# Units of a scan run by halves of the channels, with one PSUM bank for the state sum and two for B

## The chip, the core and the metric

The kernel is one program on one core of a Trainium2 chip. The core has five instruction streams that run side by side and wait for each other through semaphores: TensorE (PE, matrix products into PSUM), VectorE (DVE), ScalarE (ACT), GpSimd (POOL) and SyncE (SP, which here only starts transfers). PSUM has eight banks of 128 partitions x 512 f32. The metric is the device time of one execution in microseconds (us), less is better.

## The reference

Input x is 8 sequences of 256 tokens with 128 features. After a layer norm two branches run on it, and the output is x + s * g.

```python
x = L0_attn_x
xn = _layernorm(x, axis=-1)
s = _L0_attn_ref(xn, ...)            # the selective scan
g = _silu(_L0_ffn_ref(xn, ...))      # mixture of 8 experts, the best 2 of each token
x = x + s * g
...
# inside _L0_attn_ref: DIN = 256 channels, S = 16 states, R = 64
xz = xn @ W_in
xi, z = jnp.split(xz, 2, axis=-1)
...                                   # causal convolution of 4 taps, then silu, gives xc
dt, Bm, Cm = jnp.split(xc @ W_x, [R, R + S], axis=-1)
dt = jax.nn.softplus(dt @ W_dt + b_dt)
dA = jnp.exp(dt[..., None] * A)
dBu = (dt * xc)[..., None] * Bm[:, :, None, :]
...                                   # h = dA * h + dBu along the tokens
y = jnp.einsum('blds,bls->bld', h, Cm) + D_skip * xc
y = y * jax.nn.silu(z)
return x + y @ W_out
```

## The kernel before

**Tiling.** The 2048 tokens are cut into 4 chunks of 512 tokens (two sequences). Within a chunk the scan works on tiles of 128 partitions that hold 4 states of 32 channels. There are 8 blocks of 32 channels and 4 quads of states, so 32 such tiles in a chunk. Two neighbouring blocks make a pair, and one quad of one pair is a *unit*: 16 units in a chunk, 64 in all. Unit n belongs to chunk n // 16; `place(n)` (L101) gives its quad and its pair. Before, the pair runs fastest: the four pairs of quad 0, then the four pairs of quad 1, and so on.

**What a unit is.** ACT makes the decay `dec` = exp(dt * A) (L448, two instructions). DVE multiplies `rep` (dt * u of these channels, repeated over the four states) with B of this quad, which lies in a PSUM bank `pB` (L726, `times_B`), and runs the scan (L735) into `hs`. POOL multiplies with C (L358, two instructions) into `hc`; PE adds the four states up into the bank of the channels, `py` (L837, `reduce`, for two units at a time), after a product of xc with D_skip has opened the sum (L826, `skip_xc`). When all units of a chunk are added, DVE multiplies `py` with silu(z) (L744, `gate_y`), and PE multiplies with W_out (L920, job "o").

**Around it** lie the jobs of the next chunk's front (transpose "tr", convolution "xc0", "xc1", gate input "z0", "z1", the product "dt", then "v0", "v1" for dt, the softplus on ACT, DVE and POOL, and the normalised input "tn"), and the eight experts of the mixture: "m" jobs (L908), "y" jobs (L914), emptied by ACT (L531) and added by POOL (L411), a few of them by DVE (L761: expert 4 of chunk 2 and experts 6 and 7 of chunk 3). The router of the mixture is a chain of small DVE instructions (L668 to L696) that ends in `score`; job "gs" on PE (L896) waits for it, and job "gb" and the expert outputs stand behind it.

**The order is written out by hand.** Every engine runs through the same numbered slots: slot 2n is `times_B` of unit n on DVE and slot 2n+1 its scan; a chunk is 32 slots. The tables FIRST, MIDDLE, LAST and STEPS say in which slot of a chunk which job or DVE step is issued; "slot 16 of chunk 1" below means 16 slots after the chunk's first. Each engine is strictly in order, so what waits holds up all that stands behind it. PE runs `reduce` six slots after the units that it adds (LAG).

**Banks.** `pB` has one bank, `pdbu` (the output of `times_B`) two, `py` two (one for each half of the channels), the jobs three. B of a quad is spread by one PE product (L816, `spread_B`), which must wait until DVE has made the last `times_B` of the quad before, and the next `times_B` waits for it.

**The repeated rows.** `rep` has one buffer. SP writes it by 32 transfers a chunk (L336), eight for each pair, as soon as the last quad of the old chunk has read that pair, and only once dt * u of all 256 channels is there (`far_done`, released by the memset at L716). Ahead of them SP writes the C rows out and reads them back in (L318, L323). ACT and DVE wait for a pair's transfers at its first quad.

**The end.** After the last scan DVE adds the two last experts' outputs, with `gate_y` of chunk 3 between them; then come "o" on PE and three DVE instructions (L754, L797, L799).

## Time and profile before

| | |
|---|---|
| runs (3) | median 395.79 us, 393.49 to 396.25 |
| the profiled execution | 393.58 us |
| its span in the profile | 391.6 us |
| mean granted TensorE clock | 0.873 of full |
| busy | PE 287.7 us, DVE 314.6, ACT 214.2, POOL 228.1 |

The profile follows one execution. Its span runs from the first to the last instruction and is 2.0 us shorter than that execution's own time. Times in rows are microseconds from the start of the span. A share of busy time is a mean over stages with different limits; whether a stage is bound by an engine is read from the waits in it.

### The profile page before, as it was taken

Reading aid. Unit: us, or ns where it says so; the run is one execution under the profiler, and the core shown is the slowest. Engines: PE = TensorE matmul, PEld = TensorE weight load, DVE = VectorE, ACT = ScalarE, POOL = GpSimd, SP = SyncE. Lnnn points to the kernel's source line nnn. Section 1 sums busy time; section 2 is a strip of 40 time slices with the busy share of each in tenths; the row PEclk is TensorE's granted clock in tenths of the full one; section 3 lists DMA queues with packets and bytes.
Section 4 is the critical chain, followed back from the end, with each engine's and each line's share of the span. In section 5 each row is a group of like instructions: output and inputs, shape, how many; then the busy total and the mean of one; then the engine's idle time right before and its main releaser. Section 6 shows DMA issues by size and latency. Waiting matters only on the chain. (4 is left out here: it accounts for less than half of the span.)

```text
span 391.6 us, 4141 instructions
## 1 busy us (share of the span) xinstructions
PE 287.7 (73%) x1191; PEld 147.4 (38%) x1191; DVE 314.6 (80%) x374; ACT 214.2 (55%) x405; POOL 228.1 (58%) x197
## 2 busy tenths in 40 slices
PE   0847077969258878877669969877489869698884
PEld 0313043424224354224426445224236346063453
DVE  3772378693999899997897998997985998999955
ACT  1271264597444744588627664589526563656840
POOL 3050221853953965646757866546946676769880
PEclk9986569978688999988969978989859998879999
DMA  6945940004003870004004950003003980000001
GB/s 179 263 104 122 206 109 2 1 0 110 1 1 74 200 157 2 1 10 100 2 1 102 206 122 1 1 20 92 0 2 79 205 202 0 0 0 2 0 0 55
DMA packets 16755, 26.74 MB, mean 68 GB/s; under 512 B 4263, under 2 KB 9758, under 8 KB 16734
## 3 DMA queue, kind: packets, MB, share of 16 engines
q1 hardware_dynamic: 16438, 25.96, 28.4%
q10 hardware_dynamic: 296, 0.53, 0.4%
q8 instruction: 10, 0.16, 0.2%
q14 instruction: 11, 0.09, 0.1%
HBM read 8.52 MB, written 1.18 MB: 25 GB/s over the span
## 5 line engine op out<-in xcount | busy, mean ns | idle before, releaser
L358 POOL TENSOR_TENSOR hc<-hs,Ct 128x512 f32<-128x512 f32 x126 | 160.2, 1295 | 72.3 <-DVE hs L735 72.3
L735 DVE TENSOR_TENSOR_SCAN hs<-dec,pdbu 128x1024 f32<-128x1024 f32 x64 | 146.2, 2284 | 4.5
L448 ACT ACTIVATE dec<-rep,negA 128x512 f32<-128x512 f32 x128 | 88.6, 722 | 42.3 <-DMA rep<-dt_u 30.6
L726 DVE TENSOR_TENSOR pdbu<-rep,pB 128x1024 f32<-128x1024 f32 x64 | 78.5, 1227 | 32.3 <-PE pB L816 21.1
L908 PE MATMUL px<-xnT,w 128*128 128x512 f32 x128 | 71.8, 668 | 17.2 <-ACT hT L542 13.6
L914 PEld LDWEIGHTS px<-w,hT 128*128 128x128 f32 x512 | 68.3, 212 | 29.0 <-issue 12.3
L914 PE MATMUL px<-w,hT 128*128 128x128 f32 x512 | 70.9, 298 | 9.5 <-DVE glc L669 7.5
L411 POOL TENSOR_TENSOR acc<-acc,ysc 128x512 f32<-128x512 f32 x29 | 37.5, 1292 | 47.7 <-ACT ysc L531 38.8
L542 ACT ACTIVATE hT<-px,cols 128x512 f32<-128x512 f32 x64 | 43.7, 689 | 22.5 <-PE px L908 19.1
L531 ACT ACTIVATE ysc<-px,score 128x128 f32<-128x128 f32 x116 | 33.1, 367 | 39.5 <-PE px L914 36.7
L837 PE MATMUL py<-hc,rsel 128*32 128x512 f32 x256 | 47.5, 668 | 8.2 <-POOL hc L358 8.2
L908 PEld LDWEIGHTS px<-xnT,w 128*128 128x128 f32 x128 | 23.7, 210 | 47.1 <-issue 20.7
L873 PE MATMUL px<-xrT,wtap 128*128 128x512 f32 x56 | 27.1, 614 | 0.0
L816 PE MATMUL pB<-dtp,sel 128*128 128x512 f32 x32 | 19.9, 706 | 6.7 <-DVE pdbu L726 6.7
L880 PE MATMUL px<-xc,wx 128*96 128x512 f32 x16 | 12.1, 900 | 11.4 <-ACT xc L464 11.4
L837 PEld LDWEIGHTS py<-hc,rsel 128*32 128x32 f32 x256 | 6.6, 113 | 36.0 <-POOL hc L358 23.1
L920 PE MATMUL px<-wout,sz 128*128 128x128 f32 x64 | 11.9, 362 | 9.8 <-DVE sz L744 9.8
L873 PEld LDWEIGHTS px<-xrT,wtap 128*128 128x128 f32 x56 | 10.5, 196 | 15.7 <-issue 13.2
L920 PEld LDWEIGHTS px<-wout,sz 128*128 128x128 f32 x64 | 11.0, 267 | 11.7 <-issue 7.3
L365 POOL TENSOR_TENSOR zr<-zr,xv 128x512 f32<-128x512 f32 x6 | 7.8, 1294 | 12.2 <-DVE xv L707 12.2
L816 PEld LDWEIGHTS pB<-dtp,sel 128*128 128x128 f32 x32 | 5.9, 207 | 20.3 <-issue 12.8
L704 DVE TENSOR_SCALAR xv<-ev 128x512 f32<-128x512 f32 x8 | 4.4, 552 | 9.9 <-ACT ev L473 9.8
(103 smaller groups left out, 251.0 us busy)
## 6 DMA issues: line engine op xcount, KB each, us to landing
rep<-dt_u SPq DMA_DIRECT2D x128, 128.0 KB, 2.4
Ct<-c_rows SPq DMA_DIRECT2D x16, 256.0 KB, 4.7
w<-in_L_ffn_W SPq DMA_DIRECT2D x1, 1024.0 KB
out<-xn SPq DMA_DIRECT2D x4, 256.0 KB, 3.2
x_sb<-in_L_attn_x SPq DMA_DIRECT2D x1, 768.0 KB, 5.4
hc<-in_L_attn_conv_w ACTq DMA_DIRECT2D x1, 512.0 KB, 4.3
x_sb<-in_L_attn_x SPq DMA_DIRECT2D x1, 256.0 KB, 5.4
win<-in_L_attn_W_in SPq DMA_DIRECT2D x1, 256.0 KB, 4.7
```

The lines of the kernel that those rows point to most:

```text
L358: eng.tensor_tensor(hc[:, n % HC_RING, i, :], hs[:, n % HS_RING, i, :], Ct[:, k % 2, j, :], ALU.mult).then_inc(hc_last if n == UNITS - 1 e ...
L411: pool.tensor_tensor(acc[:, k % 3, :], acc[:, k % 3, :], ysc[:, :], ALU.add).then_inc(acc_added, 1)
L448: act.activation(dec[:, n % DEC_RING, i, :], rep[:, q, 0, :], ACT.Exp, scale=negA[:, q, j:j + 1])\
L531: ins = act.activation(ysc[:, t], src[:, t], ACT.Copy, scale=score[:, k % 2, i, e:e + 1])
L542: ins = act.activation(hT[:, e % 2, b, :], src[:, :], ACT.Relu, bias=cols[:, V_B1 + HB * e + b:V_B1 + HB * e + b + 1])
L726: dve.tensor_tensor(pdbu[:, :, :], rep[:, 2 * pair:2 * pair + 2, 1, :], pB[:, :, :].to_broadcast([P, 2, CH]), ALU.mult).then_inc(dbu_done, 1)
L735: dve.tensor_tensor_scan(hs[:, n % HS_RING].rearrange("p b t -> p (b t)"), dec[:, n % DEC_RING].rearrange("p b t -> p (b t)"), pdbu[:, :, ...
L816: pe.matmul(pB[:, 0, :], sel[:, j].rearrange("p s d -> p (s d)"), dtp[:, k % 2, :], start=True, stop=True)\
L837: last = pe.matmul(py[r:r + GD, b, :], rsel[:, :], hc[:, n % HC_RING, i, :], start=False, stop=j == QUADS - 1)
L873: last = pe.matmul(dst[:, :], wtap[:, t, b * P:(b + 1) * P], xrT[:, :, t:t + SEQ], start=t == 0, stop=t == TAPS - 1)
L908: last = pe.matmul(dst[:, :], w1[:, e, b * P:(b + 1) * P], xnT[:, k % 2, :], start=True, stop=True)
L914: last = pe.matmul(dst[:, i * D:(i + 1) * D], hT[:, e % 2, b, i * P:(i + 1) * P], w2[:, e, b, :], start=b == 0, stop=b == HB - 1)
```

## The change

The units of a chunk are put in another order: first the four quads of states over pairs 0 and 1 (channels 0 to 127), then the four quads over pairs 2 and 3. With it:

- one `py` bank holds the sum of the half that is being worked on; it is opened by one L826 product for each half and read by one `gate_y` for each half, in slots 20 and 36 instead of one in slot 35. A line that is now issued for the second half waits until `gate_y` of the first half has read the bank;
- the bank that came free goes to `pB`, which has two. B is spread for every two units instead of every four (32 instead of 16 products), and one turn earlier: the product for the units from slot 4i+8 on stands in slot 4i+3;
- the memset that releases `far_done` is made for each half, and SP asks for each pair only for its own half; pairs 0 and 1 are free for the next chunk after the 8th unit, pairs 2 and 3 after the 16th.

The line numbers in rows are those of the kernel before; after the change the same instructions stand at L820 (`spread_B`), L828, L839, L748 (`gate_y`), L719 (memset).

```diff
@@ -29,6 +29,8 @@
 BLOCKS = DIN // GD
 PAIRS = BLOCKS // 2
 PER_CHUNK = QUADS * PAIRS
+PER_HALF = PER_CHUNK // DB
+HALF_PAIRS = PAIRS // DB
 UNITS = CHUNKS * PER_CHUNK
 HALF = 2 * PER_CHUNK
 DEC_RING, HS_RING, HC_RING = 3, 3, 4
@@ -75,14 +77,14 @@
 
 STEPS = [{
     "silu": [13], "log1p": [15, 15], "correct": [16, 16, 16, 16], "sum_dt": [15, 15], "times_dt": [18, 21],
-    "scale_rows": [4], "normalise": [14], "gate": [19, 20, 20, 20, 21, 21], "gate_e": [19], "gate_y": [35],
+    "scale_rows": [4], "normalise": [14], "gate": [19, 20, 20, 20, 21, 21], "gate_e": [19], "gate_y": [20, 36],
 }, {
     "silu": [12], "log1p": [15, 15], "correct": [16, 16, 17, 19], "sum_dt": [16, 20], "times_dt": [18, 21],
     "scale_rows": [4], "normalise": [11], "gate": [19, 20, 20, 20, 20, 20], "gate_e": [20], "finish": [20],
-    "gate_y": [35],
+    "gate_y": [20, 36],
 }]
 START = {"gate": [1, 1, 1, 3, 3, 3], "gate_e": [0]}
-END = {"gate_y": [35]}
+END = {"gate_y": [20, 36]}
 LEAD = 2
 LAG = 6
 
@@ -100,7 +102,8 @@
 
 def place(n):
 
-    return n // PER_CHUNK, n // PAIRS % QUADS, n % PAIRS
+    k, b = n // PER_CHUNK, n // PER_HALF % DB
+    return k, n // HALF_PAIRS % QUADS, HALF_PAIRS * b + n % HALF_PAIRS
 
 
 def by_dve(job, k):
@@ -204,9 +207,9 @@
         def banks(name, n):
             return ctx.enter_context(nc.psum_tensor(name, [P, n, CH], F32))
 
-        pB = banks("pB", 1)
+        pB = banks("pB", 2)
         pdbu = banks("pdbu", 2)
-        py = banks("py", DB)
+        py = banks("py", 1)
         px = [banks(f"px{i}", 1)[:, 0, :] for i in range(AUX)]
 
 
@@ -326,8 +329,10 @@
 
             def repeat_dt_u(k, pair):
 
+                sp.wait_ge(far_done, DB * k + pair // HALF_PAIRS + 1)
                 if k > 0:
-                    free = PER_CHUNK * (k - 1) + PAIRS * (QUADS - 1) + pair + 1
+                    b = pair // HALF_PAIRS
+                    free = PER_CHUNK * (k - 1) + PER_HALF * (b + 1) - HALF_PAIRS + pair % HALF_PAIRS + 1
                     sp.wait_ge(decay_done, 2 * free)
                     sp.wait_ge(dbu_done, free)
                 for q in (2 * pair, 2 * pair + 1):
@@ -337,7 +342,6 @@
 
             for k in range(CHUNKS):
                 repeat_C(k)
-                sp.wait_ge(far_done, k + 1)
                 for pair in range(PAIRS):
                     repeat_dt_u(k, pair)
             for k in range(CHUNKS):
@@ -507,7 +511,7 @@
                 elif job == "dt":
                     if k >= 2:
                         act.wait_ge(c_out, 16 * (k - 1))
-                        act.wait_ge(B_spread, QUADS * (k - 1))
+                        act.wait_ge(B_spread, DB * QUADS * (k - 1))
                     ins = act.activation(dtp[0:RANK + 2 * STATES, k % 2, :], src[0:RANK + 2 * STATES, :], ACT.Copy)
                 elif job in ("v0", "v1"):
                     b = int(job[1])
@@ -711,19 +715,19 @@
                 dve.wait_ge(dt_done, DB * k + b + 1)
                 wait_silu(dve, "xc", k, b)
                 dve.tensor_tensor(dt_u[:, b, 1, :], dt_u[:, b, 0, :], xc[:, k % 2, b], ALU.mult).then_inc(u_done, 1)
-                if b == DB - 1:
-                    dve.wait_ge(u_done, DB * (k + 1))
-                    dve.memset(dt_u[:, :, 0, 0:CH:SEQ], FAR).then_inc(far_done, 1)
+                dve.wait_ge(u_done, DB * k + b + 1)
+                dve.memset(dt_u[:, b, 0, 0:CH:SEQ], FAR).then_inc(far_done, 1)
 
             def times_B(n):
 
                 k, j, pair = place(n)
-                dve.wait_ge(B_spread, n // PAIRS + 1)
+                m = n // HALF_PAIRS
+                dve.wait_ge(B_spread, m + 1)
                 if j == 0:
                     dve.wait_ge(rep_in[pair], N_REP * (k + 1))
                 if n > 0:
                     dve.wait_ge(scan_done, n)
-                dve.tensor_tensor(pdbu[:, :, :], rep[:, 2 * pair:2 * pair + 2, 1, :], pB[:, :, :].to_broadcast([P, 2, CH]),
+                dve.tensor_tensor(pdbu[:, :, :], rep[:, 2 * pair:2 * pair + 2, 1, :], pB[:, m % 2:m % 2 + 1, :].to_broadcast([P, 2, CH]),
                                   ALU.mult).then_inc(dbu_done, 1)
 
             def scan(n):
@@ -737,11 +741,11 @@
                                        pdbu[:, :, :].rearrange("p b t -> p (b t)"), 0.0, ALU.mult, ALU.add)\
                     .then_inc(scan_done, 1)
 
-            def gate_y(k):
-
-                dve.wait_ge(reduced, PER_CHUNK // 2 * (k + 1))
-                wait_silu(dve, "z", k, DB - 1)
-                dve.tensor_tensor(sz[:, k % 2], py[:, :, :], sz[:, k % 2], ALU.mult).then_inc(yg_done, 1)
+            def gate_y(k, b):
+
+                dve.wait_ge(reduced, (PER_CHUNK * k + PER_HALF * (b + 1)) // 2)
+                wait_silu(dve, "z", k, b)
+                dve.tensor_tensor(sz[:, k % 2, b], py[:, 0, :], sz[:, k % 2, b], ALU.mult).then_inc(yg_done, 1)
 
             def empty(job, k):
 
@@ -776,8 +780,8 @@
                     scan(n // 2) if n % 2 else times_B(n // 2)
                 if n == 2 * UNITS - 1:
                     times_C(dve, UNITS - 1)
-                for k, _ in steps_at(n, "gate_y"):
-                    gate_y(k - 1)
+                for k, b in steps_at(n, "gate_y"):
+                    gate_y(k - 1, b)
                 for k, _ in steps_at(n, "scale_rows"):
                     scale_rows(k)
                 for k, _ in steps_at(n, "normalise"):
@@ -808,33 +812,31 @@
 
             def spread_B(m):
 
-                k, j = m // QUADS, m % QUADS
+                k, j = m // (DB * QUADS), m % QUADS
+                if m % (DB * QUADS) == 0:
+                    wait_emptied(pe, "dt", k)
+                if m > 1:
+                    pe.wait_ge(dbu_done, HALF_PAIRS * (m - 1))
+                pe.matmul(pB[:, m % 2, :], sel[:, j].rearrange("p s d -> p (s d)"), dtp[:, k % 2, :], start=True, stop=True)\
+                    .then_inc(B_spread, 1)
+
+            def skip_xc(k, b):
+
+                wait_silu(pe, "xc", k, b)
+                if DB * k + b > 0:
+                    pe.wait_ge(yg_done, DB * k + b)
+                pe.matmul(py[:, 0, :], skip[:, b, :], xc[:, k % 2, b, :], start=True, stop=False)
+
+            def reduce(m):
+
+                k, j, pair = place(2 * m)
                 if j == 0:
-                    wait_emptied(pe, "dt", k)
-                if m > 0:
-                    pe.wait_ge(dbu_done, PAIRS * m)
-                pe.matmul(pB[:, 0, :], sel[:, j].rearrange("p s d -> p (s d)"), dtp[:, k % 2, :], start=True, stop=True)\
-                    .then_inc(B_spread, 1)
-
-            def skip_xc(k):
-
-                for b in range(DB):
-                    wait_silu(pe, "xc", k, b)
-                if k > 0:
-                    pe.wait_ge(yg_done, k)
-                for b in range(DB):
-                    pe.matmul(py[:, b, :], skip[:, b, :], xc[:, k % 2, b, :], start=True, stop=False)
-
-            def reduce(m):
-
-                k, j, pair = place(2 * m)
-                if j == 0 and pair == 0:
-                    skip_xc(k)
+                    skip_xc(k, pair // HALF_PAIRS)
                 for n in (2 * m, 2 * m + 1):
                     pe.wait_ge(hc_last, 2) if n == UNITS - 1 else pe.wait_ge(hc_done, 2 * (n + 1))
                     for i in range(2):
-                        b, r = divmod((2 * (n % PAIRS) + i) * GD, P)
-                        last = pe.matmul(py[r:r + GD, b, :], rsel[:, :], hc[:, n % HC_RING, i, :], start=False,
+                        r = (2 * n + i) * GD % P
+                        last = pe.matmul(py[r:r + GD, 0, :], rsel[:, :], hc[:, n % HC_RING, i, :], start=False,
                                          stop=j == QUADS - 1)
                 last.then_inc(reduced, 1)
 
@@ -914,8 +916,8 @@
                             last = pe.matmul(dst[:, i * D:(i + 1) * D], hT[:, e % 2, b, i * P:(i + 1) * P], w2[:, e, b, :],
                                              start=b == 0, stop=b == HB - 1)
                 else:
-                    pe.wait_ge(yg_done, k + 1)
                     for b in range(DB):
+                        pe.wait_ge(yg_done, DB * k + b + 1)
                         for i in range(TPC):
                             last = pe.matmul(dst[:, i * D:(i + 1) * D], sz[:, k % 2, b, i * P:(i + 1) * P], wout[:, b, :],
                                              start=b + i == 0, stop=(b, i) == (DB - 1, TPC - 1))
@@ -927,9 +929,10 @@
             pe.wait_ge(setup, N_SETUP)
             pe.wait_ge(vec_c, 1)
             spread_B(0)
+            spread_B(1)
             for n in range(END_SLOT + 1):
-                if n % (2 * PAIRS) == 2 * PAIRS - 1 and n // (2 * PAIRS) + 1 < CHUNKS * QUADS:
-                    spread_B(n // (2 * PAIRS) + 1)
+                if n % 4 == 3 and n // 4 + 2 < UNITS // HALF_PAIRS:
+                    spread_B(n // 4 + 2)
                 if n % 4 == 2 and 0 <= (n - LAG) // 4 < UNITS // 2:
                     reduce((n - LAG) // 4)
                 for job, k in SLOTS.get(n, []):
```

Three places of the resulting order. On DVE at the start, before the first unit (dt_u<-dt_u,xc is dt * u of a half), before:

```order
L713 TENSOR_TENSOR dt_u<-dt_u,xc 128x512
L704 TENSOR_SCALAR xv<-ev 128x512
L707 TENSOR_TENSOR xv<-xv,ev 128x512
L365 TENSOR_TENSOR zr<-zr,xv 128x512
L371 TENSOR_TENSOR dt_u<-zr,rl 128x512
L713 TENSOR_TENSOR dt_u<-dt_u,xc 128x512
L716 MEMSET dt_u 128x2x2
```

and after the change:

```order
L717 TENSOR_TENSOR dt_u<-dt_u,xc 128x512
L719 MEMSET dt_u 128x2
L708 TENSOR_SCALAR xv<-ev 128x512
L711 TENSOR_TENSOR xv<-xv,ev 128x512
L369 TENSOR_TENSOR zr<-zr,xv 128x512
L375 TENSOR_TENSOR dt_u<-zr,rl 128x512
L717 TENSOR_TENSOR dt_u<-dt_u,xc 128x512
L719 MEMSET dt_u 128x2
```

The memset of the first half has moved ahead of the five instructions of the second half.

On PE in chunks 1 and 2, from the transpose of `score` (job "gs") to the expert product "y4"; before:

```order
L896 MATMUL px2<-ident,score 32x128
L837 MATMUL py<-hc,rsel 32x512 x4
L908 MATMUL px0<-xnT,w1 128x512
L902 MATMUL px1<-b2d,sT 128x512
L914 MATMUL px2<-w2,hT 128x128 x8
L908 MATMUL px0<-xnT,w1 128x512
L816 MATMUL pB<-dtp,sel 128x512
L914 MATMUL px1<-w2,hT 128x128 x8
```

and after:

```order
L898 MATMUL px2<-ident,score 32x128
L828 MATMUL py<-xc,skip 128x512
L839 MATMUL py<-hc,rsel 32x512 x4
L910 MATMUL px0<-xnT,w1 128x512
L904 MATMUL px1<-b2d,sT 128x512
L916 MATMUL px2<-w2,hT 128x128 x8
L910 MATMUL px0<-xnT,w1 128x512
L820 MATMUL pB<-dtp,sel 128x512
L916 MATMUL px1<-w2,hT 128x128 x8
```

The product with D_skip of the second half stands between `score` and the expert outputs now, and the spread at this place serves units two turns later; another spread (slot 27) stands a little further on, ahead of y4.

On DVE at the very end, before:

```order
L358 TENSOR_TENSOR hc<-hs,Ct 128x512 x2
L761 SCALAR_TENSOR_TENSOR acc<-px,score,acc 128x128 x4
L744 TENSOR_TENSOR sz<-py,sz 128x1024
L761 SCALAR_TENSOR_TENSOR acc<-px,score,acc 128x128 x4
L754 TENSOR_TENSOR xn<-px,xn 128x512
```

and after:

```order
L362 TENSOR_TENSOR hc<-hs,Ct 128x512 x2
L765 SCALAR_TENSOR_TENSOR acc<-px,score,acc 128x128 x8
L748 TENSOR_TENSOR sz<-py,sz 128x512
L758 TENSOR_TENSOR xn<-px,xn 128x512
L801 TENSOR_TENSOR xn<-xn,acc 128x512
```

The last `gate_y` is half as wide and stands behind both expert sums instead of between them.

## Rows read from the trace of the kernel before

**Rows 1.** Page, busy time, share of the span and instructions of each engine
```profile
PE 287.7 (73%) x1191; PEld 147.4 (38%) x1191; DVE 314.6 (80%) x374; ACT 214.2 (55%) x405; POOL 228.1 (58%) x197
```

**Rows 2.** Waits of the run: total us, times, longest us
```profile
ACT dec L448 <- DMA rep<-dt_u: 30.6, 12, 6.9
...
DVE pdbu L726 <- PE pB L816: 21.1, 10, 5.2
```

**Rows 3.** Timeline, DVE, the start: start us, duration us, instruction, [idle before <- releaser]
```profile
28.41 0.69 DVE L713 TENSOR_TENSOR dt_u<-dt_u,xc 128x512 f32<-128x512 f32 x1
...
32.48 0.06 DVE L716 MEMSET dt_u<- 128x4 f32 x1
39.61 1.23 DVE L726 TENSOR_TENSOR pdbu<-rep,pB 128x1024 f32<-128x1024 f32 x1 [7.06 <-DMA rep<-dt_u]
...
50.55 0.19 DVE L673 TENSOR_REDUCE gsm<-gex 128x4 f32<-128x32 f32 x1 [6.99 <-ACT gex L549]
```

**Rows 4.** Timeline, ACT, the start
```profile
44.58 1.33 ACT L448 ACTIVATE dec<-rep,negA 128x512 f32<-128x512 f32 x2 [3.65 <-DMA rep<-dt_u]
...
50.31 0.21 ACT L549 ACTIVATE gex<-glc 128x32 f32<-128x32 f32 x1
```

**Rows 5.** Timeline, DVE, chunk 0 and the first unit of chunk 1
```profile
92.00 1.23 DVE L726 TENSOR_TENSOR pdbu<-rep,pB 128x1024 f32<-128x1024 f32 x1 [3.93 <-PE pB L816]
95.84 0.43 DVE L704 TENSOR_SCALAR xv<-ev 128x512 f32<-128x512 f32 x1 [2.60 <-ACT ev L473]
...
136.29 1.23 DVE L726 TENSOR_TENSOR pdbu<-rep,pB 128x1024 f32<-128x1024 f32 x1 [1.36 <-PE pB L816]
```

**Rows 6.** Timeline, PE, chunk 1: a spread, the reduce of slot 18
```profile
155.82 1.02 PE L816 MATMUL pB<-dtp,sel 128*128 128x512 f32 x2
...
182.11 1.29 PE L837 MATMUL py<-hc,rsel 128*32 128x512 f32 x8
```

**Rows 7.** Timeline, DVE, chunk 1
```profile
178.47 0.43 DVE L704 TENSOR_SCALAR xv<-ev 128x512 f32<-128x512 f32 x1 [2.60 <-ACT ev L473]
...
188.52 1.22 DVE L726 TENSOR_TENSOR pdbu<-rep,pB 128x1024 f32<-128x1024 f32 x1
...
208.05 1.23 DVE L726 TENSOR_TENSOR pdbu<-rep,pB 128x1024 f32<-128x1024 f32 x1 [2.62 <-PE pB L816]
...
230.19 1.20 DVE L744 TENSOR_TENSOR sz<-py,sz 128x1024 f32<-128x1024 f32 x1
```

**Rows 8.** Timeline, PE, chunk 1 from "gs" to the next "tr"
```profile
198.96 0.37 PE L896 MATMUL px<-ident,score 128*32 128x128 f32 x1 [6.95 <-DVE score L696]
199.26 1.94 PE L837 MATMUL py<-hc,rsel 128*32 128x512 f32 x8
...
226.88 1.06 PE L837 MATMUL py<-hc,rsel 128*32 128x512 f32 x8
231.53 3.76 PE L920 MATMUL px<-wout,sz 128*128 128x128 f32 x16 [3.58 <-DVE sz L744]
...
237.99 0.60 PE L856 MATMUL px<-ident,rl 128*128 128x128 f32 x4
```

**Rows 9.** Timeline, DVE, chunk 2 behind `score`
```profile
297.35 1.23 DVE L726 TENSOR_TENSOR pdbu<-rep,pB 128x1024 f32<-128x1024 f32 x1 [5.22 <-PE pB L816]
...
305.90 1.12 DVE L761 SCALAR_TENSOR_TENSOR acc<-px,score,acc 128x128 f32<-128x128 f32 x4
```

**Rows 10.** Timeline, PE: "y4" of chunk 2, slot 22 of chunk 3
```profile
302.64 1.95 PE L914 MATMUL px<-w,hT 128*128 128x128 f32 x16
...
358.23 1.05 PE L837 MATMUL py<-hc,rsel 128*32 128x512 f32 x4 [1.41 <-POOL hc L358]
```

**Rows 11.** Timeline, DVE, the end
```profile
382.96 1.21 DVE L744 TENSOR_TENSOR sz<-py,sz 128x1024 f32<-128x1024 f32 x1
384.90 1.13 DVE L761 SCALAR_TENSOR_TENSOR acc<-px,score,acc 128x128 f32<-128x128 f32 x4 [0.72 <-PE px L914]
386.68 0.69 DVE L754 TENSOR_TENSOR xn<-px,xn 128x512 f32<-128x512 f32 x1 [0.66 <-PE px L920]
```

2 lines of the change are left out of this document (1 added, 1 removed).

## The prediction, made before the changed kernel was run

> **What bounds the kernel now.** I read the page first: DVE is the busiest engine, busy for 314.6 us of 391.6 [rows 1]. It is idle for 77.0 us, so the table of waits comes next. It shows 21.1 us, in 10 waits, in which the next `times_B` waits for the spread of B, and 30.6 us in which ACT waits for repeated rows [rows 2]. The second is no wait of DVE: after the start DVE never stands for a decay, so hiding the repeated rows in mid-run earns nothing by itself.
>
> The first is no sum to be cashed in either. Each wait has to be looked at in the timeline: who is late there, and what comes next. At the start the bound is the transfers. SP may not start them before the memset at 32.48; pair 0 lands at 39.61 [rows 3], pair 1 at 44.58 [rows 4], so 5.0 us a pair. Then ACT stands before a decay of pair 2 and cannot reach the small exponential of the router, which ends the 6.99 us wait of DVE at 50.55 [rows 3, 4]. In slots 4 to 16 of every chunk the bound is the front of the next chunk on PE and ACT: DVE, wherever it waits for B there, waits once more at L704 for the result of that front [rows 5, 7]. From L704 to `score` DVE itself is the bound and PE waits for it, 6.95 us before "gs" [rows 8]. From `score` to `gate_y` PE runs without a pause and DVE is ahead of it by little. The last 20 us are PE with POOL and ACT.
>
> **The change, part by part.** The sum is made against the profiled execution, 393.58 us.
>
> *Start.* The first half's dt * u ends at 28.41 + 0.69 = 29.10 [rows 3], and the memset follows it: far_done for pairs 0 and 1 comes 32.48 - 29.17 = 3.3 us earlier. The five DVE instructions that the memset has passed belong to the second half, whose transfers start third. Pairs 0 and 1 land at about 36.3 and 41.3. The first four units use only these two, so ACT does not stand for pair 2: after pair 1 it makes two decays (1.33 us) [rows 4] and the first of the next unit (half of that), and reaches the router's exponential at 41.3 + 1.3 + 0.7 = 43.3 instead of 50.31 [rows 4]. **7.0 us earlier**, and DVE, POOL and PE, which all stood behind this, move with it. PE gets one spread more before the expert jobs, 1.02 us [rows 6], double if the clock is low, which the waits there hide. If the transfers land no earlier because others are still under way, 3.3 of the 7.0 go; the C rows started just before make that possible.
>
> *Chunk 0, rest.* The wait of 3.93 at 92.00 disappears, but 2.60 at L704 follows it right behind [rows 5], and grows by the same amount: the front of chunk 1 sets it. In that front PE gets one spread more (slot 11) and one product with D_skip less (slot 6, now one half), the same shape and price: 0. Then DVE is the bound up to chunk 1. The wait of 1.36 at 136.29 [rows 5] goes. `gate_y` costs 1.20 [rows 7] for 1024 columns; for 512 columns of PSUM with a second operand the nearest row is 0.69 [rows 11], so the half in slot 36 saves 0.5 and the half in slot 20 adds 0.7, with 0.1 for the second memset: **-1.1**.
>
> *Chunk 1.* Slots 4 to 16: the front is the bound again, 0. Up to `score`, DVE is, and the half `gate_y` stands before the router's chain: +0.8. From `score` on the wait of 2.62 [rows 7] ends, so DVE would be 2.6 ahead. But PE runs through from 198.96 to 226.88 + 1.06 = 227.9 [rows 8] and now has the product with D_skip and the spread of slot 27 in it: 2 x 1.02. The sum is complete at 229.9, `gate_y` of the half ends at 230.6, half of "o" (half of 3.76, since the first half's products no longer wait) at 232.5, then y7, which with "o" took the 6.46 from 231.53 to 237.99 [rows 8], 2.9 without it: "tr" starts at 235.4 instead of 237.99, -2.6. Together **-1.8**.
>
> *Chunk 2.* Up to `score` +0.8. Here the wait for B is 5.22 and the next to be late is known: L761 needs y4, which PE ends at 302.64 + 1.95 = 304.6; DVE comes to it at 305.90 [rows 9, 10]. PE has the same two additions ahead of y4, 2.0 us: L761 starts at 306.6. All of the 5.22 is given back, and 0.7 more. At the end of the chunk the half `gate_y` and half of "o" win these 0.7 again. Together **+0.8**.
>
> *Chunk 3.* No front. At 358.23 PE waits 1.41 for POOL [rows 10]; a spread (slot 19) and the product with D_skip stand ahead of that now, 2.0: **+0.5**, on a chain of PE, ACT and POOL that goes on to the end.
>
> *End.* Before, `gate_y` was made at 382.96, between the expert sums. Now it waits for the last one, 384.90 + 1.13 = 386.03, and takes 0.69; PE's second half of "o" follows, 1.0 us (half of its 16 records), so L754 starts at about 387.9 instead of 386.68 [rows 11]: **+1.2**.
>
> Sum: -7.0 - 1.1 - 1.8 + 0.8 + 0.5 + 1.2 = **-7.4**. The profiled execution would be 386.2; the median shown is 2.2 above it, so the forecast for the median is 395.8 - 7.4 = 388.4.
>
> **Costed at nothing.** The repeated rows of chunks 1 to 3 are moved under the work of the units before: pairs 0 and 1 are asked for from slot 18 on and needed 14 slots later; at 5.0 us a pair they have ten and more to spare. Pairs 2 and 3 have eight units. SP is then not behind on its C rows, which come before the repeated rows as they did. The other added spreads (slots 3, 11 and 19) stand in front of waits of PE: 3.58 before "o", 6.95 before "gs" [rows 8]. If PE came without these waits, each would cost 1.0.
>
> What is unknown is the length of PE's run from `score` on. After its wait of 6.95 the clock is down: eight records take 1.94 where they later take 1.06 [rows 8]. If the two additions fall into that part they cost twice their price, +2.0 in each of chunks 1 and 2; if PE keeps its clock, because its waits are shorter, some 2 us in each are won.
>
> **Rivals.**
>
> *Everything that DVE waits for B is won.* For it: DVE is the busiest engine [rows 1], and the bank is double now. Against it: the L704 waits and y4. If both gave way, 21.1 [rows 2] + 7.0 less 0.7 for the halves of `gate_y` would be won: 368.4. The Trainium skill, Perfetto Trace Analysis, section Identifying the Most-Contended Engine, says that improving a kernel generally means improving its busiest engine, and takes occupancy as the measure; by that rule the time would be this one. This trace does not bear it out: its DVE rows show the next late one behind each of those waits. 0.04. A part of it (376 to 382), where PE's run is shorter than I read it: 0.12.
>
> *PE becomes the bound.* 16 spreads more are 16 x 1.02 = 16.3 us [rows 6]. I put 3 of them on the path, with the products that D_skip moves. If half of them are, 8.2 us, the gain is gone: about 396. For it: PE's run behind `score` is already as long as DVE's. Against it: 9.5 us of waits before "gs" and before "o" in chunk 1 alone. 0.20.
>
> *PE stops for the one bank of the sum, and it gets slower.* In slot 22 PE must not open the sum of the second half before `gate_y` of slot 20 has read the first; that waits for the reduce of slot 18. Before, the reduce ends at 182.11 + 1.29 = 183.4 [rows 6] and slot 20's `times_B` at 188.52 + 1.22 = 189.7 [rows 7], 6.3 us later. From the point at which the reduce comes more than 6.3 us later, DVE stands, then PE, at a low clock. Priced by the longest wait for a bank that there is, 5.22 [rows 9], in three chunks: 15.7 - 7.4, so 404. Against it: PE waits for `score`, later in DVE's order than `gate_y`, anyway. 0.06.
>
> *The start does not move*, because the transfers land no earlier or another thing ends ACT's stop: 3.3 to 7.0 less, 391.7 to 395.4. 0.08.
>
> **Numbers.** The forecast with its bounds (PE's clock, 4 us either way) is 384 to 392.5: 0.50. About 1%, 4 us, is what a measurement of this kernel tells from no change, its three runs being 2.8 apart. Below 391.8 lie all but a little of the forecast, the faster rivals and a sliver of the last: 0.66. Within 1%: 0.25. Slower: 0.09, the bank and the worse half of PE as the bound. The range leaves out 1 in 10 at each end: 379 to 397.
>
> **What would show it.** Right: the first `times_B` at 36.3 and the router's exponential near 43.3; no wait for B anywhere; waits at L704 longer than 2.60 in chunks 0 to 2, by what the waits for B before them were; in chunk 2 a wait of L761 for y4 of about 4 us; the end some 1.2 us longer behind y6. Wrong: if L704's waits stay at 2.60, the front follows DVE and more is won than I say; if DVE waits for PE in L744 of slot 20, or PE for it in L826, the third rival holds.

## The result

| | runs | median us | lowest to highest |
|---|---|---|---|
| before | 4 | 395.7 | 393.49 to 396.25 |
| changed | 4 | 382.9 | 381.1 to 383.8 |

The ratio is 0.9681, with a 95% interval of 0.9629 to 0.9732: the change makes the kernel 12.8 us faster. The forecast was 388.4, with a range of 379 to 397; the sum was 7.4 us. Direction and range hold, the size is 5.5 us short. An execution more than 1.5% above the fastest of its kernel is left out of the medians and ratios below; there is one, of the kernel "order only".

The profiled execution of the changed kernel took 381.1 us, its span is 379.1, its mean granted TensorE clock 0.908 (before: 393.58, 391.6, 0.873).

### The profile page after: what moved, and what is told of

Its sections match the earlier page's. It is cut to its first block, busy times and chain, and to the rows that moved or that the text cites. A ratio compares the mean times of both kernels' runs of the same rounds, so it can differ in the third digit from the quotient of the medians.

```text
span 379.1 us, 4220 instructions
## 1 busy us (share of the span) xinstructions
PE 291.9 (77%) x1223; PEld 146.8 (39%) x1223; DVE 314.9 (83%) x382; ACT 214.1 (56%) x405; POOL 228.1 (60%) x197
## 4 chain that ended last, share of the span: by engine, by line
PE 37%; DVE 27%; POOL 12%; issue 9%; ACT 9%; SPq 2%; DMA 2%; DVEq 0%; POOLq 0%; ACTq 0%
DVE hs L739 11%; POOL hc L362 9%; PE px L875 7%; PE px L916 6%; PE py L839 5%; DVE pdbu L730 4%; PE px L910 4%; PE pB L820 4%; PE px L882 3%; DVE rl L622 2%; SPq L341 2%; PE px L864 2%; PE py L828 2%; POOL acc L415 2%; ACT ysc L535 2%
## 5 line engine op out<-in xcount | busy, mean ns | idle before, releaser
L452 ACT ACTIVATE dec<-rep,negA 128x512 f32<-128x512 f32 x128 | 88.2, 723 | 16.1 <-DVE hs L739 8.7
L910 PE MATMUL px<-xnT,w 128*128 128x512 f32 x128 | 68.7, 640 | 10.7 <-ACT hT L546 7.2
L916 PEld LDWEIGHTS px<-w,hT 128*128 128x128 f32 x512 | 65.6, 205 | 22.7 <-issue 11.3
L916 PE MATMUL px<-w,hT 128*128 128x128 f32 x512 | 67.9, 290 | 3.2 <-ACT hT L546 1.7
L839 PE MATMUL py<-hc,rsel 128*32 128x512 f32 x256 | 44.3, 654 | 5.7 <-POOL hc L362 5.7
L820 PE MATMUL pB<-dtp,sel 128*128 128x512 f32 x64 | 38.2, 685 | 12.0 <-DVE pdbu L730 10.9
L820 PEld LDWEIGHTS pB<-dtp,sel 128*128 128x128 f32 x64 | 12.1, 210 | 32.8 <-DVE pdbu L730 18.5
L708 DVE TENSOR_SCALAR xv<-ev 128x512 f32<-128x512 f32 x8 | 4.4, 553 | 19.2 <-ACT ev L477 19.1
L839 PEld LDWEIGHTS py<-hc,rsel 128*32 128x32 f32 x256 | 6.4, 113 | 34.7 <-POOL hc L362 20.7
L875 PEld LDWEIGHTS px<-xrT,wtap 128*128 128x128 f32 x56 | 10.5, 197 | 16.2 <-issue 13.7
L622 DVE TENSOR_SCALAR rl<-x_sb,mv,rr 128x128 f32<-128x128 f32 x16 | 11.1, 756 | 1.8 <-POOL rr L398 1.8
L922 PE MATMUL px<-wout,sz 128*128 128x128 f32 x64 | 9.3, 295 | 3.5 <-DVE sz L748 3.5
```

Of the source, the lines that this page charges most:

```text
L452: act.activation(dec[:, n % DEC_RING, i, :], rep[:, q, 0, :], ACT.Exp, scale=negA[:, q, j:j + 1])\
L820: pe.matmul(pB[:, m % 2, :], sel[:, j].rearrange("p s d -> p (s d)"), dtp[:, k % 2, :], start=True, stop=True)\
L839: last = pe.matmul(py[r:r + GD, 0, :], rsel[:, :], hc[:, n % HC_RING, i, :], start=False, stop=j == QUADS - 1)
L875: last = pe.matmul(dst[:, :], wtap[:, t, b * P:(b + 1) * P], xrT[:, :, t:t + SEQ], start=t == 0, stop=t == TAPS - 1)
L910: last = pe.matmul(dst[:, :], w1[:, e, b * P:(b + 1) * P], xnT[:, k % 2, :], start=True, stop=True)
L916: last = pe.matmul(dst[:, i * D:(i + 1) * D], hT[:, e % 2, b, i * P:(i + 1) * P], w2[:, e, b, :], start=b == 0, stop=b == HB - 1)
```

## The profile after

The page's line of busy times, the answer to [rows 1]:

```profile
PE 291.9 (77%) x1223; PEld 146.8 (39%) x1223; DVE 314.9 (83%) x382; ACT 214.1 (56%) x405; POOL 228.1 (60%) x197
```

No engine has less to do. The gain is all idle time: DVE idles 64.2 us of 379.1 instead of 77.0 of 391.6. Which idle time went is in the table of waits (total us, times, longest us), the answer to [rows 2]:

```profile
DVE xv L708 <- ACT ev L477: 19.1, 4, 8.9
...
DVE acc L765 <- PE px L916: 9.3, 3, 4.6
...
ACT dec L452 <- DMA rep<-dt_u: 7.2, 2, 3.7
```

The same two waits in the kernel before:

```profile
DVE xv L704 <- ACT ev L473: 9.8, 4, 2.6
DVE acc L761 <- PE px L914: 5.3, 2, 4.6
```

The 21.1 us for B are gone from the list altogether. But the wait for the next chunk's front (L704 before, L708 now) has grown from 9.8 to 19.1, and that for expert outputs (L761, now L765) from 5.3 to 9.3. The timeline of DVE shows where (start us, duration us, instruction, idle before and its releaser); these rows answer to those of [rows 3, 5, 7, 9, 11]:

```profile
29.08 0.06 DVE L719 MEMSET dt_u<- 128x2 f32 x1
36.19 1.23 DVE L730 TENSOR_TENSOR pdbu<-rep,pB 128x1024 f32<-128x1024 f32 x1 [3.62 <-DMA rep<-dt_u]
...
43.30 0.18 DVE L677 TENSOR_REDUCE gsm<-gex 128x4 f32<-128x32 f32 x1 [3.15 <-ACT gex L553]
...
87.13 0.43 DVE L708 TENSOR_SCALAR xv<-ev 128x512 f32<-128x512 f32 x1 [8.94 <-ACT ev L477]
...
136.23 4.55 DVE L622 TENSOR_SCALAR rl<-x_sb,mv,rr 128x128 f32<-128x128 f32 x4
...
170.81 0.43 DVE L708 TENSOR_SCALAR xv<-ev 128x512 f32<-128x512 f32 x1 [4.80 <-ACT ev L477]
...
292.39 1.13 DVE L765 SCALAR_TENSOR_TENSOR acc<-px,score,acc 128x128 f32<-128x128 f32 x4 [2.89 <-PE px L916]
...
371.23 1.13 DVE L765 SCALAR_TENSOR_TENSOR acc<-px,score,acc 128x128 f32<-128x128 f32 x4 [1.85 <-PE px L916]
372.27 0.68 DVE L748 TENSOR_TENSOR sz<-py,sz 128x512 f32<-128x512 f32 x1
374.20 0.69 DVE L758 TENSOR_TENSOR xn<-px,xn 128x512 f32<-128x512 f32 x1 [1.25 <-PE px L922]
```

The first `times_B` comes at 36.19 and the router's exponential 7.2 us earlier than before: the start is as worked out. The wait at 87.13 is 8.94 where 3.93 + 2.60 stood before, that at 292.39 is new and stands for y4. And on PE in chunk 1, the answer to [rows 8]:

```profile
140.93 0.63 PE L858 MATMUL px<-ident,rl 128*128 128x128 f32 x4 [3.34 <-DVE rl L622]
...
142.56 1.91 PE L828 MATMUL py<-xc,skip 128*128 128x512 f32 x2
...
189.90 0.37 PE L898 MATMUL px<-ident,score 128*32 128x128 f32 x1 [6.28 <-DVE score L700]
190.06 2.00 PE L828 MATMUL py<-xc,skip 128*128 128x512 f32 x2
...
217.39 1.06 PE L839 MATMUL py<-hc,rsel 128*32 128x512 f32 x8
...
219.35 1.05 PE L922 MATMUL px<-wout,sz 128*128 128x128 f32 x8
220.68 1.16 PE L922 MATMUL px<-wout,sz 128*128 128x128 f32 x8 [0.27 <-DVE sz L748]
...
225.02 0.63 PE L858 MATMUL px<-ident,rl 128*128 128x128 f32 x4 [1.40 <-DVE rl L622]
```

Here is what the sum did not have. From "gs" to the end of the last `reduce` PE took 28.98 us before (198.96 to 227.94) and takes 28.55 now (189.90 to 218.45), with two products more in it. Instead of two products longer it is as long as before (28.42 and 28.58 in the second traces of the two kernels). One reason stands in PE's rows of the kernel before:

```profile
216.95 2.11 PE L837 MATMUL py<-hc,rsel 128*32 128x512 f32 x8
...
220.56 1.10 PE L816 MATMUL pB<-dtp,sel 128*128 128x512 f32 x2 [0.45 <-DVE pdbu L726]
```

That run was not unbroken. A `reduce` took 2.11 us, because its second half waited for POOL's `hc`, where the same one takes 1.06 in the changed kernel, and the spread behind it stood 0.45 for DVE. The added products fill such standing time.

The first-half products of "o" then run while the second half is still being gated, so the 3.58 before "o" has shrunk to 0.27. Before, the granted clock was at 0.50 behind that wait from 230.7 to 237.5, and "o" took 3.76 and y7 3.08. In the changed kernel it stays at 1.00 there; the halves of "o" take 1.05 and 1.16 and y7 takes 1.95.

**Where the 12 us are.** The table sets the starts of the same instructions in the two profiled executions beside each other, and the change in each stage's length. Both kernels were profiled a second time (runs "before again" and "after again" below), and the last columns are means over two traces each.

| event | before, at us | after, at us | stage changed by | mean of two | forecast |
|---|---|---|---|---|---|
| router's exponential read (L673, L677) | 50.55 | 43.30 | -7.25 | -7.2 | -7.0 |
| L704, L708 of chunk 0 | 95.84 | 87.13 | -1.46 | -1.2 | 0 |
| "tr" in chunk 1 | 149.86 | 140.93 | -0.22 | +0.3 | -1.1 |
| L704, L708 of chunk 1 | 178.47 | 170.81 | +1.27 | +1.3 | 0 |
| "gs" in chunk 1 | 198.96 | 189.90 | -1.40 | -0.7 | +0.8 |
| "tr" in chunk 2 | 237.99 | 225.02 | -3.91 | -3.4 | -2.6 |
| L704, L708 of chunk 2 | 266.57 | 253.65 | +0.05 | 0.0 | 0 |
| "gs" in chunk 2 | 285.65 | 274.27 | +1.54 | +1.5 | +0.8 |
| y4 of chunk 2 added (L761, L765) | 305.90 | 292.39 | -2.13 | -2.1 | +0.7 |
| y6 of chunk 3 added | 381.92 | 368.25 | -0.16 | -1.0 | -0.2 |
| L754, L758 | 386.68 | 374.20 | +1.19 | +1.2 | +1.2 |

(The forecast's -0.2 is its -0.7 for the end of chunk 2 and +0.5 for chunk 3.) Before rounding the means add up to -11.2, the forecast's to -7.4. What is left of the 12.8 lies in how single executions differ: two traces of the same kernel are up to 1.7 us apart in one stage (chunk 3 of before: 76.02 and 77.63; from the exponential to L708 in the changed kernel: 43.83 and 45.50).

## The experiments

The theory after this comparison: the start is the earlier memset and the order of pairs; B's second bank earns only what L704 and y4 leave; and the part that was not forecast comes from PE's clock behind its long wait before "gs". The rivals: the second bank earns all of the 12.8 less the start (5.6 us), or the order of halves itself does. The comparisons ran beside runs of the kernel before, whose medians there were 394.06, 393.47 and 395.38 us.

### The start: release and order apart

Changed kernel, chunk 0's two halves released together (label "one release"):

```diff
                 dve.tensor_tensor(dt_u[:, b, 1, :], ...).then_inc(u_done, 1)
+                if k == 0 and b == 0:
+                    return
                 dve.wait_ge(u_done, DB * k + b + 1)
-                dve.memset(dt_u[:, b, 0, 0:CH:SEQ], FAR).then_inc(far_done, 1)
+                for h in (range(DB) if k == 0 else [b]):
+                    dve.memset(dt_u[:, h, 0, 0:CH:SEQ], FAR).then_inc(far_done, 1)
```

Expected:

> The changed kernel, but in chunk 0 the rows of both halves are released together, after the second half's dt * u, as before the change. Theory A (the start is bound by the transfers, then by the order of pairs): the first times_B moves from 36.2 back to 39.5, the router's exponential from 43.05 to 46.4, and all behind it by the same 3.3 us; the time is 382.9 + 3.3 = 386.2. The other 4.0 us of the start's gain stay, because they come from the units' order (no pair 2 before the router's exponential). Theory B (the early release carries the whole start): 7.2 us are lost, 390.1. Theory C (something further on has slack for it): under 1 us is lost.

Measured: 388.03 us (384.43 to 388.2), ratio to before 0.9808 (0.9742 to 0.9874). Its trace, DVE:

```profile
39.70 1.23 DVE L733 TENSOR_TENSOR pdbu<-rep,pB 128x1024 f32<-128x1024 f32 x1 [7.01 <-DMA rep<-dt_u]
...
46.81 0.19 DVE L677 TENSOR_REDUCE gsm<-gex 128x4 f32<-128x32 f32 x1 [3.16 <-ACT gex L553]
```

And the other way round, the kernel before with the release by halves alone ("early release"):

```diff
             def repeat_dt_u(k, pair):
+                sp.wait_ge(far_done, DB * k + pair * DB // PAIRS + 1)
...
-                sp.wait_ge(far_done, k + 1)
...
-                if b == DB - 1:
-                    dve.wait_ge(u_done, DB * (k + 1))
-                    dve.memset(dt_u[:, :, 0, 0:CH:SEQ], FAR).then_inc(far_done, 1)
+                dve.wait_ge(u_done, DB * k + b + 1)
+                dve.memset(dt_u[:, b, 0, 0:CH:SEQ], FAR).then_inc(far_done, 1)
```

> The kernel before, with one part of the change alone: each half's rows are released by a memset of their own, and SP asks for a pair as soon as its half is there. Order of the units and banks are as before. Theory A: pairs 0 and 1 land 3.3 us earlier, and as SP issues without a break pairs 2 and 3 do too; the first times_B moves from 39.6 to 36.3, the router's exponential from 50.3 to 47.0, and the time from 395.7 to 392.4. Theory B (the early release needs the halves' order to be worth anything): no change.

Measured: 392.25 (390.38 to 394.05), ratio 0.9948 (0.9912 to 0.9983). DVE:

```profile
36.21 1.23 DVE L725 TENSOR_TENSOR pdbu<-rep,pB 128x1024 f32<-128x1024 f32 x1 [3.58 <-DMA rep<-dt_u]
...
47.19 0.19 DVE L673 TENSOR_REDUCE gsm<-gex 128x4 f32<-128x32 f32 x1 [7.03 <-ACT gex L549]
```

The 7.2 us of the start are now two prices that agree from both sides. The release: 46.81 - 43.30 = 3.5 when it is taken away, 50.55 - 47.19 = 3.4 when it comes alone. The order of pairs, under which ACT does not stand for pair 2 before the router: 50.55 - 46.81 = 3.7. The wait of 7.03 in the last row is that stop of ACT, untouched by an earlier start. In the medians the release is worth 1.2 (alone; 2 by the ratio) and 5.1 (taken away), since the stages behind it vary: from the exponential to L708 took 46.8 us in "one release" and 43.8 in the changed kernel's first trace (45.5 in its second). That "early release" lies at the expected 392.4 is in part chance: the expectation was counted from 395.7, and the kernel before took 393.47 beside it.

### The second bank for B alone

Changed kernel with the banks as before: one for B, two for the sum ("order only"). The core of it:

```diff
-        pB = banks("pB", 2)
+        pB = banks("pB", 1)
...
-        py = banks("py", 1)
+        py = banks("py", DB)
...
-                if m > 1:
-                    pe.wait_ge(dbu_done, HALF_PAIRS * (m - 1))
+                if m > 0:
+                    pe.wait_ge(dbu_done, HALF_PAIRS * m)
...
-                if n % 4 == 3 and n // 4 + 2 < UNITS // HALF_PAIRS:
-                    spread_B(n // 4 + 2)
+                if n % 4 == 3 and n // 4 + 1 < UNITS // HALF_PAIRS:
+                    spread_B(n // 4 + 1)
```

> The halves' order alone: py keeps two banks (one for each half, so that no product waits for the other half's gate_y), pB has one, B is spread for every two units right after the second of them. Theory A (the second bank of B is what removes DVE's waits, but a part of them only replaces waits for the front): DVE waits for B at most of the 31 changes; where PE stands idle the product fits under the scan, where PE is busy it costs 1 to 5 us. I expect 25 to 40 us of such waits, about 12 of them in place of the waits at L708, and a time of 395 to 410, slower than before the change. Theory B (the order, with its earlier transfers, is the gain): the time stays within 4 us of 382.9. The start up to the router's exponential should be as in the changed kernel under both.

Measured: 386.21 (383.71 to 388.69, without one execution of 390.7), ratio 0.9792 (0.9698 to 0.9886). Theory A failed: the kernel is 8.8 us too fast for its lower end, with fewer waits for B than it said. By its time it is theory B, 3.3 us from the changed kernel. The waits:

```profile
DVE pdbu L730 <- PE pB L820: 21.9, 8, 4.4
DVE xv L708 <- ACT ev L477: 9.9, 4, 2.6
DVE acc L765 <- PE px L916: 6.3, 2, 4.4
```

DVE stands for B in 8 of 31 turns (10 of 15 before), longest in PE's run behind "gs" of chunk 1, where other jobs stand ahead of the spread (4.44 us at 201.06). The rest of the table is the kernel before again: L708 9.9 and L765 6.3. So the pair of kernels "order only" and changed isolates the second bank: it removes 21.9 us of waits, 19.1 - 9.9 = 9.2 return at L708 and 9.3 - 6.3 = 3.0 at L765, and the median falls by 3.3 (386.21 to 382.9), the span of the profiled executions by 5.1 or 3.4 (384.2 to 379.1 and 380.8). By the ratios it is 1.1%, 4.4 us, with intervals that still overlap: the second bank is worth some 3 to 5 us, and that it is worth anything is likely, not certain. (With the bank goes the earlier turn of each spread; the second `py` bank of "order only" earns nothing, since no D_skip product waits for a `gate_y` in the changed kernel.) Order and release together, without the bank, give 2.1%.

### The tail

```diff
-END = {"gate_y": [20, 36]}
+END = {"gate_y": [20, 35]}
```

> The changed kernel with the last gate_y one slot earlier, between the two last expert sums as before the change (slot 35 instead of 36 of chunk 3). Theory A (the end was lengthened by 1.2 us because gate_y and then half of "o" stand behind the last expert sum): L758 starts about 1.2 us earlier against the end of the reduce, 381.7. Theory B (the end is bound by PE's y7 and ACT's silu anyway): no change.

Measured: 382.18 (381.77 to 382.97), ratio 0.9695 (0.9647 to 0.9743). DVE at the end:

```profile
370.31 1.13 DVE L765 SCALAR_TENSOR_TENSOR acc<-px,score,acc 128x128 f32<-128x128 f32 x4 [4.63 <-PE px L916]
371.36 0.68 DVE L748 TENSOR_TENSOR sz<-py,sz 128x512 f32<-128x512 f32 x1
...
375.08 0.69 DVE L758 TENSOR_TENSOR xn<-px,xn 128x512 f32<-128x512 f32 x1 [0.66 <-PE px L922]
```

From y6's sum to L758 it takes 4.77, against 5.95 in the changed kernel and 4.76 before. The +1.2 of the end is shown, and it comes from the slot, not from the halves. In the median 0.7 of it can be seen, less than the runs differ.

### PE's clock behind the wait for `score`

In the changed kernel, PE makes the spread ahead of "gs" six times over while it waits there in chunks 1 and 2 ("warm"). The five repetitions write the same values again:

```diff
+HELD = (HALF + 19, 2 * HALF + 19)
...
-                pe.matmul(pB[:, m % 2, :], ...)
+                for _ in range(times):
+                    last = pe.matmul(pB[:, m % 2, :], ...)
...
                 elif job == "gs":
+                    if HALF * (k - 1) + 19 in HELD:
+                        spread_B(2 * QUADS * k - 2, 6)
```

> The changed kernel; in chunks 1 and 2 the spread of slot 19 is held back to just before the transpose of score and made six times over into the same bank with the same values, so that PE is busy in the 6.3 us in which it waits for score. Theory A (PE's run behind score is at the low clock for its first 4 to 5 us, and that lengthens it): the product with D_skip takes 1.0 instead of 2.0 and the reduce behind it 1.1 instead of 1.6 to 1.9, y4 of chunk 2 ends 1.5 to 2 us sooner after score, DVE's wait of 2.89 at L765 shrinks by as much; the time falls by 1.5 to 2.5, since chunk 1 has no wait of DVE there except through L622. Theory B (the clock of that stretch does not matter to DVE): L765's wait is shorter but the time is the same within 0.5. Theory C: six more products delay the transpose of score; then the time grows by up to 1.

Measured: 379.65 (379.44 to 379.87), ratio 0.9625 (0.958 to 0.9671), under the changed kernel by 3.3 us in the medians and 2.2 by the ratios, where 1.5 to 2.5 were expected; its slowest execution is faster than the changed kernel's fastest. PE in chunk 2:

```profile
274.78 0.28 PE L903 MATMUL px<-ident,score 128*32 128x128 f32 x1 [1.92 <-DVE score L701]
274.90 1.08 PE L831 MATMUL py<-xc,skip 128*128 128x512 f32 x2
...
288.97 1.95 PE L921 MATMUL px<-w,hT 128*128 128x128 f32 x16
```

and a window there (its bounds, its length, busy us of PE, PEld, DVE, ACT and POOL, then the granted clock, DMA share and GB/s):

```profile
275.00:277.00 2.00, 2.00 (x12) 0.40 (x11) 2.00 (x2) 0.27 (x1) 0.00 (x0) 1.00 0.00 0
```

The product with D_skip takes 1.08 instead of 2.00, the granted clock stands at 1.00 behind "gs", and y4 starts 14.2 us behind it. The same was done to the kernel before, with products into the bank of "gs" that nothing reads ("before, warm"), since there the low clock lasts longest:

```diff
                 elif job == "gs":
+                    if k in (2, 3):
+                        for _ in range(6):
+                            pe.matmul(dst[:, :], sel[:, 0]..., dtp[:, (k - 1) % 2, :], start=True, stop=True)
```

> The kernel before; in chunks 1 and 2 PE makes six products of 128x512 whose result nothing uses, into the bank of the transpose of score, while it waits for score. Theory A (in the kernel before, the run behind score was long because the clock was low, in chunk 2 for 9.6 us): the clock stays at full, y4 of chunk 2 ends some 15.5 us after score instead of 18.9, the waits for B of 2.62 and 5.22 us fall to under 1 and about 2; and so much of the change's gain could be had without it: the time falls by 3 to 6 us, to 388 to 391. Theory B (the second bank is what matters there): the waits for B stay above 2 us each, the time falls by under 2.

Measured: 390.2 (386.82 to 390.51), ratio 0.9844 (0.9767 to 0.9921). PE, then DVE:

```profile
285.46 0.28 PE L900 MATMUL px<-ident,score 128*32 128x128 f32 x1 [1.56 <-DVE score L696]
...
297.89 1.95 PE L918 MATMUL px<-w,hT 128*128 128x128 f32 x16
```

```profile
292.59 1.23 DVE L726 TENSOR_TENSOR pdbu<-rep,pB 128x1024 f32<-128x1024 f32 x1 [0.56 <-PE pB L816]
```

y4 starts 12.4 us behind "gs" instead of 17.0, and DVE waits 0.56 for B instead of 5.22 [rows 9]. So most of the longest wait for B was never a matter of banks: it was a spread at the end of a PE stretch at 1.2 GHz. That holds for this one wait; 17.5 us of waits for B are left in "before, warm". The two warm kernels also give the price of the two additions at the full clock. In chunk 2 it is 14.2 - 12.4 = 1.8, near the 2.0 of the forecast. In chunk 1 it is nothing: from "gs" to the end of the last `reduce` PE takes 27.0 us in both. In chunk 2 of the changed kernel they seem not to cost their 1.8 either: y4 starts 16.1 behind "gs" and not 17.0 + 1.8.

Why? One way is that the added products themselves end the low stretch earlier. To the kernel before, two products of 128x512 were added in the slots of the two additions ("two more"), into a job's bank that the job overwrites:

```diff
+            def one_more(n):
+                job, k = SLOTS[n][0]
+                j = JOBS.index((job, k))
+                wait_emptied(pe, *JOBS[j - AUX])
+                pe.matmul(px[j % AUX][:, :], sel[:, 0]..., dtp[:, (n // HALF) % 2, :], start=True, stop=True)
...
             for n in range(END_SLOT + 1):
+                if n in (HALF + 22, HALF + 27, 2 * HALF + 22, 2 * HALF + 27):
+                    one_more(n)
```

> The kernel before with two products of 128x512 more in PE's run behind score in chunks 1 and 2, at the places where the change puts them (one ahead of the reduce in slot 22, one ahead of y4), with results that nothing uses. Theory A (the additions themselves bring the clock up sooner: full-length products stand where PE before had short ones): the low clock in chunk 2 lasts 4 to 6 us instead of 9.6, and y4 ends no later after score than before, 18 to 19 us. Theory B (products cost their price; the clock came up sooner by the phase in which the run began): the low clock lasts 9 to 10 us, y4 ends 20.5 to 21.5 us after score, the time grows by 1 to 3 us.

Measured: 393.78 (390.57 to 395.54), ratio 0.996 (0.9924 to 0.9997): four products more, and not slower. PE, chunk 2:

```profile
288.20 0.37 PE L896 MATMUL px<-ident,score 128*32 128x128 f32 x1 [7.14 <-DVE score L696]
288.37 1.91 PE L935 MATMUL px<-dtp,sel 128*128 128x512 f32 x2
...
303.65 1.95 PE L914 MATMUL px<-w,hT 128*128 128x128 f32 x16
```

y4 starts 15.45 behind "gs", 1.5 earlier than without the two products. The windows show the clock. The kernel before, from 7 us behind its "gs":

```profile
293.00:295.00 2.00, 2.00 (x12) 2.00 (x11) 0.00 (x0) 0.00 (x0) 0.00 (x0) 0.50 0.04 8
```

"two more", 2 us behind:

```profile
290.00:292.00 2.00, 2.00 (x10) 0.50 (x10) 1.93 (x4) 0.72 (x1) 1.55 (x1) 0.74 0.00 0
```

The changed kernel, 2 us behind:

```profile
276.00:278.00 2.00, 2.00 (x9) 0.20 (x8) 1.93 (x4) 0.72 (x1) 1.48 (x1) 0.50 0.04 8
```

Read so, the clock falls to 1.2 GHz (0.50) while PE still waits for `score`, and comes back behind "gs". (The four kernels with products in that wait, "warm", "before, warm" and, further below, "all" and "best", stand at 1.00 throughout. "Later front" stands below too.)

| | chunk 1: falls ahead of "gs", us | back behind "gs", us | chunk 2: falls ahead | back behind | y4 starts behind "gs", chunk 2 |
|---|---|---|---|---|---|
| before | 2.5 | 4.3 | 3.9 | 9.8 | 17.0 |
| before again | 3.7 | 3.1 | 4.2 | 9.4 | 16.8 |
| early release | 2.6 | 4.2 | 3.9 | 9.8 | 17.0 |
| two more | 2.5 | 4.3 | 4.0 | 2.8 | 15.4 |
| changed | 3.6 | 3.2 | 2.6 | 4.2 | 16.1 |
| after again | 3.6 | 3.2 | 2.7 | 4.2 | 16.1 |
| one release | 2.9 | 3.9 | 4.2 | 6.0 | 17.0 |
| order only | 4.1 | 6.2 | 2.5 | 4.4 | 16.2 |
| tail | 2.9 | 3.9 | 4.2 | 6.1 | 17.0 |
| later front | 1.0 | 5.8 | 1.1 | 5.8 | 16.9 |

The last column follows from the one before it. The start of y4 in the warm kernel with the same products (12.4 without the additions, 14.2 with them) plus half of the time at 1.2 GHz behind "gs" gives every row within 0.4 us. For the changed kernel that is +1.8 for the products and some -2.7 for the shorter low stretch.

From fall to rise the twenty stretches have three lengths: 6.8 us in fourteen, 10.2 in three, 13.7 in three. Where the clock fell at most 3.7 us ahead of "gs", the length is 6.8 in all thirteen cases, with the additions or without. Where it fell 3.9 us or more ahead, it is 13.7 in the three traces without the additions, and 10.2 (three) or 6.8 (one) with them. So the added products do go with a shorter stretch. But the changed kernel does not need them for its short one, since its clock fell late in chunk 2. "One release" and "tail" have the same products, their clock fell early, and y4 comes at 17.0, no sooner than before. Where the clock falls late in chunk 2 (changed, after again, order only), the stage from L708 to "gs" is also 20.6 us long, and 19.1 in the others of the table up to "tail". Over both stages, L708 to y4's sum on DVE, the changed kernel takes 38.7 us, "one release" and "tail" 38.1, before 39.2 to 39.3. What the late fall gives behind "gs" had been lost ahead of it.

The second traces of both kernels, each of one execution, show how far a stage repeats:

> The kernel before, profiled once more, to see what of the difference between the two traces repeats. Theory A (PE's low clock behind score lasts some 10 us in chunk 2 whatever the execution): the granted clock from score on is at 0.5 for 10 us again, y4 ends 18.9 us after score. Theory B (it differs from one execution to the next): the low stretch lasts 4 to 5 us as in chunk 1 of the first trace, y4 ends some 3 us sooner after score, and the wait for B of 5.22 us is nearer to 3.

> The changed kernel, profiled once more, to see which stages of its first trace repeat. Theory A: the low clock behind score lasts 3 to 6 us in both chunks and y4 ends 18 to 19 us after score. The stage from tr to L708 of chunk 0, 32.8 in the first trace and 34.5 to 35.7 in other runs with the same instructions there, may come out at the longer value.

"Before again" took 392.74 us (span 390.7), with 22.5 us of waits for B in 10 and 9.4 us of low clock; "after again" 382.84 (span 380.8), with stages within 0.1 us of the first trace but for one, L708 of chunk 0 (45.50 against 43.83).

### Can what L708 gives back be had?

If L708 waits for a front that is late, DVE's steps there can come later and let units pass ("later front", from the changed kernel):

```diff
-    ... "correct": [16, 16, 16, 16], "sum_dt": [15, 15], "times_dt": [18, 21],
+    ... "correct": [20, 20, 20, 20], "sum_dt": [21, 21], "times_dt": [22, 25],
...
-    ... "correct": [16, 16, 17, 19], "sum_dt": [16, 20], "times_dt": [18, 21],
+    ... "correct": [18, 18, 19, 21], "sum_dt": [18, 22], "times_dt": [20, 23],
```

> The changed kernel with DVE's steps for the next chunk's dt put later: in chunk 0 by four slots (two units), in chunks 1 and 2 by two slots (one unit), POOL's sums with them. The computation and all other slots are the same. Theory A (what is left of DVE's idle time stands at L708, 8.94, 4.80 and 3.33 us, because the front of the next chunk is late there, and DVE has units it could do meanwhile; the repeated rows have the room since the change): up to 7.4, 3.7 and 3.3 us are won there, less what the next late one gives back (gl of PE, then PE's run behind score): the time falls by 5 to 12, to 371 to 378. Theory B (PE is the bound from tr to the reduces): DVE's waits move to gmx and gsm behind L708 and the time stays within 2 us.

Measured: 378.56 (377.52 to 379.15), ratio 0.961 (0.9559 to 0.9662), just short of that. Its waits:

```profile
DVE gsm L677 <- ACT gex L553: 9.4, 4, 4.7
DVE gmx L672 <- PE px L894: 7.4, 3, 4.1
...
DVE xv L708 <- ACT ev L477: 3.4, 2, 2.4
```

L708's wait falls from 19.1 to 3.4, but at the router's chain (gsm and gmx) DVE now stands for 16.8 us instead of 4.5. Chunk 2 is 4.4 us shorter, chunk 0 longer by 1 to 3. Then all three edits together ("all": later front, warm, tail at 35), and the same with the later front only in chunks 1 and 2 ("best"):

> Later steps for the next chunk's dt, the repeated products before score, and the last gate_y one slot earlier, all in one. If the three act at different places their gains add: 382.9 less 5 to 12 for the first, 1.5 to 2.5 for the second, 1.2 for the third, 367 to 375. If PE is the bound once DVE's waits are gone, the second grows in worth and the first shrinks; if they share one chain the sum is that of the larger.

> The changed kernel with three edits: the steps for the next chunk's dt one unit later in chunks 1 and 2 only (chunk 0 as in the changed kernel, since the later steps cost 2.8 us there), the repeated products before score, the last gate_y one slot earlier. By stages of the traces so far: first unit of chunk 1 at 127.0, chunk 1 in 83.9, chunk 2 in 83.5, the rest in 75.2, plus what lies around the span: 375 to 377. If the stages do not add (PE late in chunk 2 as in the run with all three), 378 to 380.

"All": 379.22 (378.22 to 380.61), ratio 0.9634 (0.9579 to 0.9689), a miss: the gains do not add. "Best": 377.58 (377.02 to 378.3), ratio 0.9549 (0.9486 to 0.9611), 0.6 beyond its expectation. It has the lowest median here, 5.3 us under the changed kernel and 18 under the kernel before, but its executions and those of "later front" (377.52 to 379.15) overlap, so it is not shown to be faster than that one edit alone. Its waits:

```profile
DVE xv L709 <- ACT ev L478: 13.2, 3, 9.7
DVE gmx L673 <- PE px L897: 7.0, 2, 4.1
```

Why "all" is no faster than "later front" was read from traces only. In chunk 2 of "later front" DVE waits 0.90 us for y4, in chunk 1 for no expert output. Up to y4's sum a faster PE had only that to win. In "all" the wait for y4 is gone (y4's sum starts 18.6 us behind "gs", with no wait before it), but one DVE instruction has become 1.06 us longer, in "later front" and in "all":

```profile
280.05 0.69 DVE L717 TENSOR_TENSOR dt_u<-dt_u,xc 128x512 f32<-128x512 f32 x1 [1.44 <-POOL dt_u L375]
```

```profile
280.50 1.75 DVE L718 TENSOR_TENSOR dt_u<-dt_u,xc 128x512 f32<-128x512 f32 x1 [1.46 <-POOL dt_u L376]
```

In "all" POOL starts an addition of an expert output (L416, 1.27 us) at 280.43, just ahead of it; in "later front" POOL stands idle until 281.83, since that output comes later. Chunk 1 shows the same pair, 0.69 and 1.74. The six products also leave no wait before "gs" any more, where "later front" had 3.89. The 1.2 us of the tail are met by a chunk 3 that is 1.4 longer, for a reason that stays open. No run isolates any of this.

## Why the prediction was right, and where it was short

**The start (-7.0): right**, at -7.2 in both parts, 3.5 for the release and 3.7 for ACT's stop. The rival in which the start does not move fell with it.

**The repeated rows, costed at nothing: right.** ACT's 7.2 us of waits for them are the two of the start.

**Waits for B in slots 4 to 16 are given back at the front: right.** L708's waits are 8.94, 4.80 and 3.33 where L704 had 2.60 each. The rival in which all of DVE's wait is won (368.4) fell. Its smaller part, 376 to 382 because PE's run is shorter than I read it, had 0.12; the median is 0.9 us above it, and by its mechanism it came closest to what happened. The Trainium skill, Perfetto Trace Analysis, section Identifying the Most-Contended Engine, says to optimise the engine with the highest occupancy first. Here that engine, DVE, lost 21.9 us of waits and the time fell by 3 to 5: the runs bear out about a fifth of it, and what decided was who was late next.

**The rest of chunk 0 (-1.1) and the front of chunk 1 (0): too good by some 2.7 us together**, +0.3 and +1.3. The step that failed is "then DVE is the bound up to chunk 1": four short instructions before "tr" took 4.55 us (before: 3.92, and 2.96 in its second trace), and PE, idle 3.34 us for them, fell to 1.2 GHz 1 us behind that wait, its product with D_skip at 1.91 instead of 1.0.

**PE's run from `score` on: the mis-sized term.** I read the old run as one "without a pause" and charged two products on top of it, 2.0 us in each of chunks 1 and 2, at an unchanged clock.

In chunk 1 the products cost nothing. The old run did have pauses, 0.45 for DVE and about 1.05 in a `reduce` for POOL, and at the full clock it takes 27.0 us with the additions and without. Nor does `gate_y` at the chunk's end wait for PE in either kernel: in the changed one it starts at 219.94, 1.5 us behind the complete sum. At the end I charged half of "o" and y7 at 1.9 and 2.9, read from rows at 1.2 GHz; they took 1.16 and 1.95, since the clock stays up there. Most of that is not won, since "tr" now waits 1.40 for DVE. The stage is 0.8 better than forecast (-3.4 against -2.6).

In chunk 2 the products do cost 1.8, and a shorter time at 1.2 GHz behind "gs", 4.2 us instead of 9.4 to 9.8, gives back 2.7. "gs" to y4 on PE became 0.9 shorter, and the stage is 2.8 better than forecast (-2.1 against +0.7). DVE does wait for y4, 2.89 us, as said (I gave about 4). The text had the condition ("if PE keeps its clock ... some 2 us in each are won") but not its sign as the likelier, and the clock is kept for another reason than it names: PE's wait before "gs" is nearly as long as before (6.2 to 6.3 against 7.0 to 7.2).

These 0.8 and 2.8 are the bulk of the 3.8 between the two columns; the other stages' misses, up to 1.5 each, nearly cancel. With "up to `score`" counted in, chunk 2 up to y4 is 2.0 better than forecast (-0.5 against +1.5).

**Up to `score` (+0.8 each): unsettled.** The stage L708 to "gs" has two lengths, 19.1 and 20.6 us, in kernels with and without the half `gate_y` there. The extra 0.7 us of DVE cannot be told apart from that.

**Chunk 3 (+0.5): not seen**, -1.0 on the mean, with 1.6 between two traces of before. **The end (+1.2): right to 0.1**, and "tail" gives it back.

**PE as the bound, and the one bank of the sum**: neither came. PE's product with D_skip waits for no `gate_y`, and in chunk 1 DVE's `gate_y` of slot 20 follows `times_B` without one:

```profile
180.55 1.22 DVE L730 TENSOR_TENSOR pdbu<-rep,pB 128x1024 f32<-128x1024 f32 x1
181.69 0.68 DVE L748 TENSOR_TENSOR sz<-py,sz 128x512 f32<-128x512 f32 x1
```

The 0.20 on PE as the bound went against what happened: of the added products those in chunk 1 fell into standing time, and in chunk 2 the clock gave back more than they cost.

## What to carry to other kernels

A wait on the busiest engine is worth only its distance to the next late thing; take each one in the timeline and name its successor, and sum the distances, not the waits. Count an added product in its place: look for the pauses inside the run that it joins, since it costs nothing where it fills one, and for the clock that is granted there. Harmless repetitions inside a long wait of PE can earn more (2.2 to 3.3 us here) than such products cost, as long as they end before the wait does. Release a transfer by the piece that is ready, and order the work so that an in-order engine meets its other duties before it stands for the next piece.

## What the runs showed of the hardware

- In a wait of 3.9 to 7.2 us of PE before "gs" the granted clock falls to 0.50, 1.0 to 4.2 us ahead of "gs", and comes back 2.8 to 9.8 us behind it, though PE is busy from "gs" on. From fall to rise it is 6.8, 10.2 or 13.7 us, for nearly the same instructions, and nothing in between.
- What it costs is half of the time at 1.2 GHz, within 0.4 us in ten traces.
- Six products of 128x512 inside that wait (5.31 us in "before, warm", two records each) kept it at 1.00, and left 1.56 to 1.92 us of idle in the two warm kernels.
- Four DVE instructions of 128x128 take 1.11 us at 9.07, with POOL at work on two 128x4 pieces, and 4.55 at 136.23, where POOL runs `hc` and then an addition without a break:

```profile
9.07 1.11 DVE L622 TENSOR_SCALAR rl<-x_sb,mv,rr 128x128 f32<-128x128 f32 x4 [1.78 <-POOL rr L398]
```

```profile
134.51 4.97 POOL L362 TENSOR_TENSOR hc<-hs,Ct 128x512 f32<-128x512 f32 x4
```

  The Trainium skill, SBUF — State Buffer, section SBUF: two separate sides, says that DVE and GpSimd share a pair of SBUF ports, and that a GpSimd instruction, or a DVE instruction in a mode that uses both port pairs or with two SBUF inputs, holds it for its whole length while the other blocks. The rows agree: four short instructions take about as long as four of POOL's at 1.24. That these four run in such a mode no row shows. That is 3.4 us more than the 1.1 of work, on the way to "tr".

**Open:** what decides when the clock falls ahead of "gs", and by how much the added products alone shorten the low stretch; the second bank's worth within a few us; and why chunk 3 is longer in "all" and "best", which keeps them from the sum of their parts.
